# Causal attention whose steps are taken in pairs, with products of rows 0 to 63 and rows 64 to 127 in alternation

## What is computed

```
q = rope(x @ wq.T + bq); k = rope(x @ wk.T + bk); v = x @ wv.T + bv      # 16 heads of 64
scores = q @ k.T / 8, with the entries above the diagonal masked out
x1 = layernorm(x + softmax(scores) @ v @ wo.T + bo)
```

## Time and profile before

| | |
|---|---|
| median of 3 runs | 2235.4 us (2225.62 to 2242.22) |
| profiled execution | 2232.24 us |
| its span | 2230.4 us, mean granted TensorE clock 0.830 |
| TensorE matmuls (PE) | 1479.6 us busy, 66% |
| TensorE weight loads (PEld) | 1056.8 us busy, 47% |
| VectorE (DVE) | 1426.7 us busy, 64% |
| GpSimd (POOL) | 972.3 us busy, 44% |
| ScalarE (ACT) | 877.8 us busy, 39% |

### The profile page before, as it was taken

One profiled execution on the slowest core, in us unless ns is written; L12 is line 12 of the kernel. 1 busy time (PEld: TensorE's weight loads), 2 busy tenths in 40 slices (PEclk: granted clock), 3 DMA queues, 4 the chain that ended last, 5 costly groups with the idle time before them and its releaser, 6 DMA issues. The chain is left out here.

```text
span 2230.4 us, 44815 instructions
## 1 busy us (share of the span) xinstructions
PE 1479.6 (66%) x16774; PEld 1056.8 (47%) x16948; DVE 1426.7 (64%) x3287; ACT 877.8 (39%) x1764; POOL 972.3 (44%) x1288
## 2 busy tenths in 40 slices
PE   4799999999999468877743068830426777753180
PEld 1366656656666335555542047820314555543170
DVE  4588888898896567887765035534555665754454
ACT  2244444444444245666621023310325665741330
POOL 4565475474471312233244700047134665661506
PEclk9899999999999789999965579965767887875595
DMA  2000000000000111111043112222221111104422
GB/s 88 1 9 4 10 10 4 10 9 5 10 4 6 51 22 38 28 43 33 18 139 103 51 43 68 63 55 68 69 69 32 28 46 26 27 20 134 158 69 71
DMA packets 161304, 97.11 MB, mean 44 GB/s; under 512 B 53059, under 2 KB 147821, under 8 KB 160964
## 3 DMA queue, kind: packets, MB, share of 16 engines
q1 hardware_dynamic: 154948, 82.02, 13.1%
q0 software_dynamic: 6144, 12.22, 1.8%
HBM read 52.57 MB, written 33.55 MB: 39 GB/s over the span
## 5 line engine op out<-in xcount | busy, mean ns | idle before, releaser
L644 POOL TENSOR_TENSOR own_full<-own_rot 128x512 f32<-128x512 f32 x128 | 162.7, 1271 | 159.8 <-DVE own_rot L719 148.8
L1182 POOL DMA_INDIRECT mix_got<-results,mix_fetch x96 | 95.3, 993 | 281.4 <-DMA results<-mix_yo 254.0
L746 DVE TENSOR_REDUCE cross_negmax<-cross_scores 128x4 f32<-128x512 f32 x256 | 173.9, 680 | 37.8 <-PE cross_scores L450 37.5
L266 POOL TENSOR_TENSOR cross_pl<-cross_pf,cross_ph 128x512 f16<-128x512 f32 x128 | 147.8, 1157 | 84.3 <-ACT cross_pf L577 83.9
L576 ACT ACTIVATE cross_ph<-cross_scoresT 128x512 f16<-128x512 f32 x256 | 153.0, 598 | 68.8 <-PE cross_scoresT L492 60.3
L490 PE MATMUL cross_scoresT<-cross_qk,cross_kblock 128*128 128x128 f16 x1024 | 166.0, 241 | 4.3 <-issue 1.8
L492 PE MATMUL cross_scoresT<-cross_maxT,cross_sel 128*128 128x128 bf16 x1024 | 165.7, 241 | 0.0
L636 POOL TENSOR_TENSOR own_qkl<-own_full,own_qkh 128x512 f16<-128x512 f32 x128 | 157.9, 1236 | 0.0
L577 ACT ACTIVATE cross_pf<-cross_scoresT 128x512 f32<-128x512 f32 x256 | 152.8, 597 | 0.0
L554 ACT CAST own_qkh<-own_full 128x512 f16<-128x512 f32 x128 | 79.1, 618 | 178.1 <-POOL own_full L644 177.4
L266 DVE TENSOR_TENSOR own_pl<-own_pf,own_ph 128x512 f16<-128x512 f32 x128 | 139.6, 1091 | 2.1 <-ACT own_pf L577 2.0
(11 more groups left out here) (336 smaller groups left out, 5775.5 us busy)
## 6 DMA issues: line engine op xcount, KB each, us to landing
mix_stage<-in_mix_w SPq DMA_DIRECT2D x48, 256.0 KB
cross_kblock<-cross_krows SPq DMA_DIRECT2D x64, 128.0 KB
slots<-mix_blank SPq DMA_DIRECT2D x14, 512.0 KB, 6.2
mix_xg<-slots SPq DMA_DIRECT2D x56, 128.0 KB
results<-mix_yo SPq DMA_DIRECT2D x56, 128.0 KB, 1.8
cross_xin<-after SPq DMA_DIRECT2D x16, 256.0 KB, 3.2
cross_cin<-in_ctx SPq DMA_DIRECT2D x16, 256.0 KB, 3.4
after<-cross_xout SPq DMA_DIRECT2D x64, 64.0 KB, 1.5
```

What stands on the lines that cost most here:

```text
L266: ops.tensor_tensor(pl[g][:], pf[g % 2][:], ph[g][:], ALU.subtract).then_inc(s_plow, 1)
L644: nc.gpsimd.tensor_tensor(full[g % 2][:], rot[g % 2][0][:], rot[g % 2][1][:], ALU.add)\
L746: nc.vector.tensor_reduce(negmax[bb % 2][:, HU * seat(g):HU * seat(g) + HU], scp[g % 2][:].rearrange("p (h t) -> p h t", h=HU), AX.X, ALU. ...
```

## The change

TensorE takes the units of the causal attention two at a time, g and g+1. In `slots` the `scores` events of units s+4 and s+5 both stand in even slots, and so do the `scoresT` events of units s and s+1; all engines follow this order. In TensorE's part the odd unit of a pair does nothing, and the even one issues both: first the two mask matmuls, into the two banks, and then the products in turn, one of rows 0 to 63 into the first bank and one of rows 64 to 127 into the second. The number of matmuls and their shapes stay as they were. A pair waits until both banks are free: `s_max` and `s_exp` up to `unit` where it was `unit - 1`. The cross-attention path is written out on its own and does the same as before.

```diff
-                if not last or s + LEAD < 16:
+                if own and s % 2 == 0 and (not last or s + LEAD < 16):
+                    yield "scores", *unit(s + LEAD)
+                    yield "scores", *unit(s + LEAD + 1)
+                if not own and (not last or s + LEAD < 16):
                     yield "scores", *unit(s + LEAD)
...
-                yield "scoresT", b, g
+                if not own:
+                    yield "scoresT", b, g
+                elif g % 2 == 0:
+                    yield "scoresT", b, g
+                    yield "scoresT", b, g + 1
...
+                elif what == "scores" and own:
+                    if g == 0 and bb == 0:
+                        pe.wait_ge(s_qklo, NQK * (n + 2))
+                    if g % 2:
+                        return
+                    wait(pe, s_max, unit)
+                    for t in range(2):
+                        nc.tensor.matmul(scp[t][:], ident4[:, 0:P], addmask[:, 0, :], start=True, stop=False,
+                                         skip_group_check=True)
+                    for j in range(HU):
+                        for hq, hk in ((qkh, qkl), (qkl, qkh), (qkh, qkh)):
+                            for t in range(2):
+                                r, nr, c = place(g + t, j)
+                                mm = nc.tensor.matmul(scp[t][:, j * P:(j + 1) * P], hq[q][0][r:r + nr, c, cols],
+                                                      hk[q][1][r:r + nr, c, cols], start=False,
+                                                      stop=hq is hk, skip_group_check=True)
+                                if j == HU - 1 and hq is hk:
+                                    mm.then_inc(s_scores, 1)
...
+                elif what == "scoresT" and own:
+                    if g % 2:
+                        return
+                    wait(pe, s_exp, unit)
+                    if g == 0:
+                        pe.wait_ge(s_maxT, row + 1)
+                    for t in range(2):
+                        nc.tensor.matmul(stp[t][:], addmask[:, 0, 0:P], ident4[:], start=True, stop=False,
+                                         skip_group_check=True)
+                    for j in range(HU):
+                        for hk, hq in ((qkl, qkh), (qkh, qkl), (qkh, qkh)):
+                            for t in range(2):
+                                r, nr, c = place(g + t, j)
+                                nc.tensor.matmul(stp[t][:, j * P:(j + 1) * P], hk[q][1][r:r + nr, c, cols],
+                                                 hq[q][0][r:r + nr, c, cols], start=False, stop=False,
+                                                 skip_group_check=True)
+                        for t in range(2):
+                            r, nr, c = place(g + t, j)
+                            mm = nc.tensor.matmul(stp[t][:, j * P:(j + 1) * P], sel[r:r + nr, g // 2, j, :],
+                                                  maxT[bb % 2][r:r + nr, :], start=False, stop=True,
+                                                  skip_group_check=True)
+                            if j == HU - 1:
+                                mm.then_inc(s_scoresT, 1)
```

More of the change, by code:

```diff
@@ L427, in handle @@
                         mm.then_inc(s_proj, 1)
+                elif what == "scores" and own:
[16 more added lines that the diff above has]
+                                    mm.then_inc(s_scores, 1)
                 elif what == "scores":
                     if g == 0 and bb == 0:
[L431 to L437, removed]
+                        pe.wait_ge(s_proj_free, NP * (n + 1) + NQK)
+                        pe.wait_ge(s_kblock, 16 * HU * (n + 2))
+                        if masked:
+                            pe.wait_ge(s_mask, n + 2)
                     wait(pe, s_max, unit - 1)
@@ L440, in handle @@
                     if masked:
[L441 to L462, removed]
+                        nc.tensor.matmul(out[:], ident4[:, 0:P],
+                                         addmask[q][:, bb, :].unsqueeze(1).to_broadcast([P, HU, P]),
+                                         start=True, stop=False, skip_group_check=True)
+                    mm = nc.tensor.matmul(out[:], qk[q][:, g, cols],
+                                          kblock[q][:, g, bb, :, :].rearrange("p j t -> p (j t)"),
+                                          start=not masked, stop=True, skip_group_check=True)
                     mm.then_inc(s_scores, 1)
@@ L475, in handle @@
                     if masked:
-                        msk = addmask[:, 0, 0:P] if own else addmask[q][:, bb, :]
-                        nc.tensor.matmul(out[:], msk, ident4[:], start=True, stop=False, skip_group_check=True)
+                        nc.tensor.matmul(out[:], addmask[q][:, bb, :], ident4[:], start=True, stop=False,
+                                         skip_group_check=True)
                     for j in range(HU):
                         o = out[:, j * P:(j + 1) * P]
[L480 to L493, removed]
+                        nc.tensor.matmul(o, kblock[q][:, g, bb, j, :], qk[q][:, g, cols],
+                                         start=not masked and j == 0, stop=False, skip_group_check=True)
+                        mm = nc.tensor.matmul(o, sel[:, g, j, :], maxT[bb % 2][:], start=False, stop=True,
                                               skip_group_check=True)
```

## The result

The changed kernel takes 2272.6 us (median of 4 runs, 2265.1 to 2279.9) against 2238.8 us for the kernel before in the same runs: a ratio of 1.016, 95% interval 1.010 to 1.022. It is slower by about 35 us where 50 us less was forecast. A second measurement of the same kernel gave 1.017 (1.013 to 1.021). The span of the profiled execution grew from 2230.4 to 2266.9 us.

A forecast was written before the change was run, and what follows sets the result against it. TensorE was taken as the bound, VectorE close behind and the bound after the change. Seven quads give 43 us, the last quad 6, the opening 1: 50 us less, 2185 us; own range 2150 to 2205, 8 in 10 2150 to 2245.

The forecast's parts named there:

- What bounds the kernel: Causal attention: TensorE sets the pace at about 83.4 us a quad, VectorE close behind with 74.4 us of work.
- Fewer changes of row count: TensorE's scores and scoresT: a pair shares four changes of 0.1 us, saving 0.2 us a unit, 3.2 a quad.
- Alternation: TensorE's products on alternate halves overlap: spacing falls from 56 to 31 ns, saving 11.2 us a quad.
- Rivals 2, 3 and 4: No overlap, order alone: 2213 to 2245, 13%; no overlap with bunching: 2277, 10%; 0.1 us per alternation: 2575, 5%.
- rival 3: Causal attention: no overlap, and bunching into even slots makes a quad 92 us; 2277 us, chance 10%.
- The bunching.: Even against odd slots: TensorE 41 and 28 us, VectorE about 40 and 35; TensorE's lead covers the excess.
- the stricter waits: A pair waits for both banks, last used two slots earlier: charged nothing, otherwise 0.7 us a pair, 5 a quad.
- The prediction's last sentence: If spacing halves and a quad still takes over 84 us, a round trip on VectorE, not its work, is the bound.
- What VectorE keeps: VectorE's quad in causal attention: 74.4 us work, 0.5 added, 5.0 of 11.2 us waits kept; 79.9 us, 6.1 less.
- The 0.5 us for more GpSimd work beside VectorE: VectorE's low part of the weights slows as GpSimd works more densely beside it: 0.5 us more a quad.
- Rival 1, the clock: TensorE rests in odd slots, granted clock falls to 0.90, work becomes about 76 us; half the gain, 2210, chance 12%.
- The last quad: The causal attention's quad without pieces, 53 us: TensorE loses 12.8 us of work, half taken as gain, 6 us.

The follow-up runs named there:

- e5: e1 without alternation: TensorE does all products of the even unit, then all of the odd one; 2265.1 us, ratio 1.017.
- e1: Changed kernel with the odd units' scores and scoresT events back in odd slots, TensorE still issuing alternating pairs; 2221.6 us, ratio 0.997.
- e3: Changed kernel with only the scoresT events back in a slot each, scores events still in pairs; 2227.1 us, ratio 0.998.
- e6: Changed kernel with attT (transposes and their copy) ahead of scoresT in even slots, four exponentials still in a row; 2216.9 us, ratio 0.995.
- e7: Changed kernel with the odd unit's two exponentials moved to the end of the even slot; 2237.5 us, ratio 1.004.
- e15: e9 measured again, in more rounds; 2203.1 us, ratio 0.988.
- e16: The changed kernel measured again, unedited, as base for e17 and e18; 2270.5 us, ratio 1.017.
- e17: Second run of the changed kernel with filler: three extra 512-column matmuls before each odd unit's attended products; 2246.7 us, ratio 1.007.
- e18: e6 with the same filler matmuls on TensorE as e17; 2219.6 us, ratio 0.994.
- e9: Changed kernel with the edits of e1 and e6 together; 2207.6 us, ratio 0.985.

## Why the prediction was wrong

**What bounds the kernel: right.** TensorE sets the pace, VectorE is close behind. e5 against e1 shows that TensorE's work counts: 43 us for what the alternation takes off it, where the forecast's own term had 11.2 us a quad, some 80 us in all, on TensorE.

**Fewer changes of row count: right.** The 0.1 us still stands at each, twice as rarely.

**Alternation: right, and the size a little better.** 28 ns a product where I took 31. The Trainium skill, TensorEngine Tiling (Array Packing), Key Properties, says that different tiles execute in parallel and that a change of tile does not drain the array; the trace now agrees with that half as well. Rivals 2, 3 and 4 all rested on no overlap or worse, and none of them happened. The sign came out on the slow side by a mechanism that was not among them; that rival 3 put it at 2277 us, 4 us from the measured time, is chance.

**The step that failed: "The bunching."** I went through TensorE, VectorE and GpSimd and priced the even and odd slots of the first two. ScalarE is missing. Its four exponentials, 2.07 us in a row, stand ahead of the copy on which VectorE waits in order, and that wait grew by 22.6 us in 380, from 16.9 to 39.5. I had charged the stricter waits at nothing with 0.7 us a pair as the price if their cover went; the cover held (TensorE's waits in the changed kernel have no item for scores on maxima), and the cost came from another place, the order of one engine's queue. e3, e6 and e7 show it from three sides. The prediction's last sentence names the outcome, half the spacing and a quad over 84 us, and reads it rightly as a round trip on VectorE; but no rival carries it, with a price or a chance.

**"What VectorE keeps": mis-sized in consequence.** I kept 5.0 us of waits a quad and it has 20.1. VectorE's own work did not grow (372.5 / 480 x 92.5 = 71.8 us a quad, 74.4 before): 71.8 + 20.1 is the 92.5 measured, within 0.6. Of the 3.8 us a quad of the wait for the copy I kept 2.0, as if TensorE's lateness had made the rest; what it depends on is the place of the copy in ScalarE's order. The 0.5 us for more GpSimd work beside VectorE had the wrong sign: VectorE's work is 71 to 72 us a quad in the paired kernels, e15 included, and 74.3 before.

**Rival 1, the clock: right that it falls, wrong in what it costs.** I priced it against TensorE's sum (76 us, under the 79.9 of the quad) and charged half the gain. The quads of e5, e16 and e17 show that what the clock adds to TensorE's work is in the quad whole, though TensorE is idle for over 10 us of each: some 3.5 us a quad, 24 us of the time with e17's filler, and it comes on top of a loss where I had it shrink a gain. The filler and the mended queue do not add up (e18 is no faster than e6), for with the queue mended the clock is already higher, 0.96 to 0.97 by stretch against 0.93 to 0.94. That the wait behind the queue is what lets TensorE rest, and so lowers the clock, is argued from this and not shown.

**The last quad: mis-sized.** I took 6 us off it. From VectorE's last step on the next input to the last residual sum there are 147.1 us before, 159.2 in the changed kernel and 143.1 in e15; less one quad each, 61.1, 66.7 and 60.0. So it lost 6 us in the changed kernel, and gained 1 where the rest went best.

**How much of the forecast was there.** With ScalarE's queue in order and the events spread (e9, e15) a quad takes 83.4 and 83.1 us, where 79.9 was forecast, and the block ends 21 and 25 us earlier than before, where 50 was forecast; 0.8 us of a quad is the clock's (82.3 at 1.00). VectorE's waits in e15:

```profile
DVE own_attTl L775 <- ACT own_attTh L594: 18.2, 35, 0.9
DVE own_recip L765 <- PE own_attended L385: 16.2, 22, 2.2
DVE own_xl L723 <- ACT own_xh L553: 5.1, 5, 1.0
DVE own_ysum L781 <- PE own_misc L385: 4.5, 14, 0.4
DVE own_vl L737 <- ACT own_vh L570: 1.6, 4, 0.4
DVE own_rot L731 <- PE own_proj L385: 0.8, 2, 0.5
```

They are 46.4 us in 380, 10.1 a quad, where I kept 5.0. The wait for attended, which I let go altogether, is 16.2 us and was 19.5: with TensorE ahead in its sum, it is still late at that place. Spreading the events has also brought a wait that neither the kernel before nor the changed one has: TensorE's pair of scores waits for the odd unit's maximum, now taken a slot later, 15.5 us in 380 in e1, 9.1 in e9 and 6.9 in e15. Which link of the round trip holds the rest stays open.

## What to carry to other kernels

Where all engines follow one list of events, moving an event in it moves it on every engine: before pairing or bunching anything, write down for each engine what then stands ahead of the first result that another engine waits for, the lightly loaded engines too. ScalarE was busy 44% of the middle of this block before and 40% after, and the order of its work still made the larger part of the loss. And when work is taken off TensorE, read the granted clock of the same stretch after, and price a lower clock by what it adds to TensorE's work, not by whether TensorE's sum still has room. The version to use of those tried here is e9: pairs and alternation on TensorE, one event a slot for everyone else, attT ahead of scoresT in even slots, 0.985 (0.978 to 0.992) and, as e15, 0.988 (0.983 to 0.992) of the time before.

## What the runs showed of the hardware

Products of 64 rows on alternate halves of the array, into different banks, start two every 57 ns with 128 columns each, weight loads included, at granted clock 1.00 (changed kernel). A change between 64 and 128 rows costs 0.1 us. Quads of the same work took 89.2 us at a granted clock of 1.00, 90.6 at 0.98 and 92.3 at 0.96 (e5), as much longer as TensorE's matmuls were. The one thing I had not expected: 0.64 us of useless matmuls a pair lifted the granted clock from 0.93 and 0.94 to 1.00 and made the changed kernel 24 us faster (e17 against e16), so that an engine's waste was cheaper there than its rest.
